# A message-passing kernel whose per-edge products go from split fp32r matmuls to plain fp32 matmuls in four row strips

## The reference

```python
xs = concat([x[src, :8], x[dst, :8]])                  # 16 scalars an edge
xv = concat([x[src, 8:], x[dst, 8:]]).reshape(E, 16, 3)  # 16 vectors an edge
y1, y2 = sph(edge_vec)
h = 2**.5 * relu(emb @ W1 / 10**.5)                    # 10 -> 16
w = (h @ W2 / 16**.5).reshape(E, 7, 16, 8)             # seven 16 x 8 weight blocks of each edge
s_out, g_out, v_out = sums of xs, xv, y1, y2 against the blocks of w
edge_ftr = concat([TG * tanh(s_out), TG * tanh(g_out) * v_out]) * norm
x = layernorm(x + segment_sum(edge_ftr, dst))
x = layernorm(x + attention_sum(x, src, dst))          # second layer
```

## Time and profile before

| | us |
|---|---|
| median of 3 runs | 5801.54 |
| span of the profiled execution | 4918.3 |
| what lies around the span (difference) | 883 |
| TensorE busy, share of the span | 80% |
| VectorE busy | 68% |
| GpSimd busy | 70% |
| ScalarE busy | 34% |

### The profile page before, as it was taken

The page is one execution under the profiler, slowest core; times in us unless marked ns, Lnnn a source line. Parts: engine busy times, 40 slices in busy tenths (PEclk is TensorE's granted clock), DMA queues, the critical chain, the costliest instruction groups (busy, mean ns, idle before and its releaser), DMA issues. The chain is left out here.

```text
span 4918.3 us, 76839 instructions
## 1 busy us (share of the span) xinstructions
PE 3925.7 (80%) x22447; PEld 2433.8 (49%) x22447; DVE 3366.4 (68%) x5756; ACT 1665.0 (34%) x3062; POOL 3457.8 (70%) x3515
## 2 busy tenths in 40 slices
PE   0007999999999999999999600899999999999950
PEld 0004555545544555555555300677777777777740
DVE  4517999999999999999999540455555555555532
ACT  3005666666665666666666300001010100001000
POOL 5777777777666666666663177677777777777766
PEclk9999999999999999999999855899999999999975
DMA  9412222222222222222221000222222222222211
GB/s 327 135 35 50 46 44 45 44 44 46 47 44 43 43 43 43 43 43 43 49 46 30 21 11 14 55 48 46 45 48 48 45 47 49 49 49 49 49 27 25
DMA packets 266830, 253.17 MB, mean 51 GB/s; under 512 B 182298, under 2 KB 237026, under 8 KB 263867
## 3 DMA queue, kind: packets, MB, share of 16 engines
q1 hardware_dynamic: 157118, 174.83, 13.1%
q0 software_dynamic: 109024, 72.30, 9.5%
q10 hardware_dynamic: 462, 4.00, 0.3%
HBM read 160.55 MB, written 90.34 MB: 51 GB/s over the span
## 5 line engine op out<-in xcount | busy, mean ns | idle before, releaser
L626 POOL DMA_INDIRECT edge<-xp_d,idx x1440 | 1437.2, 998 | 634.6 <-issue 358.5
L1231 POOL DMA_INDIRECT gxb<-tab_d,idxb x1200 | 1290.6, 1075 | 376.6 <-issue 324.9
L890 DVE TENSOR_TENSOR prod<-G_ps,hid 128x1000 f32<-128x1000 f32 x1200 | 1385.5, 1192 | 67.0 <-ACT hid L685 39.1
L782 PE MATMUL G_ps<-FT,wst 64*128 64x500 f32 x4800 | 937.9, 434 | 38.2 <-DVE prod L890 38.2
L1266 PE MATMUL G_ps<-tb,hot 125*126 125x500 f32 (+1 forms) x3200 | 675.5, 364 | 333.0 <-DVE hotk L1288 299.7
L792 PE MATMUL R_ps<-prod,red 128*32 128x500 f32 x4800 | 769.4, 601 | 0.0
L1266 PEld LDWEIGHTS G_ps<-tb,hot 125*126 125x126 f32 x3200 | 546.3, 192 | 449.1 <-issue 349.8
L782 PEld LDWEIGHTS G_ps<-FT,wst 64*128 64x128 f32 x4800 | 421.6, 187 | 467.1 <-issue 263.9
L766 PE MATMUL T_ps<-ident,HL 125*128 125x125 f32 x3200 | 519.0, 285 | 129.1 <-DVE HL L880 128.4
L679 ACT ACTIVATE FT<-T_ps 128x500 fp32r<-128x500 f32 x800 | 470.0, 590 | 204.5 <-PE T_ps L766 192.6
L766 PEld LDWEIGHTS T_ps<-ident,HL 125*128 125x128 f32 x3200 | 332.7, 141 | 411.6 <-issue 274.4
(11 more groups left out here) (247 smaller groups left out, 4636.9 us busy)
## 6 DMA issues: line engine op xcount, KB each, us to landing
xd_d<-zeros SPq DMA_DIRECT2D x16, 1562.5 KB, 29.0
y_d<-zrb SPq DMA_DIRECT2D x40, 595.0 KB
edge<-xp_d,idx POOLq DMA_INDIRECT x1440
xv<-xd_d SPq DMA_DIRECT2D x40, 560.0 KB
y_d<-zr SPq DMA_DIRECT2D x40, 560.0 KB
edge<-sel_d SPq DMA_DIRECT2D x40, 546.9 KB
gxb<-tab_d,idxb POOLq DMA_INDIRECT x1200
em<-in_edge_attr SPq DMA_DIRECT2D x40, 175.0 KB
```

Source lines behind the costliest of these rows:

```text
L626: nc.gpsimd.indirect_dma_start(out=edge_c[:, i, 8:8 + DIM], out_offset=None, in_=xp_d, in_offset=bass.IndirectOffsetOnAxis(col, 0)).then_i ...
L782: last = Tn.matmul(G_ps[(k * 3 + i) % 2][:, a * 512:a * 512 + GW], wst[a * 64:(a + 1) * 64, (2 * i + l) * 128:(2 * i + l + 1) * 128], FT[k ...
L890: V.tensor_tensor(prod[k][i][:, :].rearrange("p (a e) -> p a e", a=2), gv, hid[k][:, :].rearrange("p (a e) -> p a e", a=1).broadcast_to([1 ...
L1231: nc.gpsimd.indirect_dma_start(out=gx[h][:, c * T1:(c + 1) * T1], out_offset=None, in_=tab_d, in_offset=bass.IndirectOffsetOnAxis(idx[h][: ...
```

## The change

The products and the MLP layer become plain fp32 matmuls. A transposed group now has 128 rows: four strips of 32, of which the fourth repeats the first input tile (`high` copies three tiles, then tile 0 once more, and `low` is gone). So a group needs four transposes for eight and one copy `out_of_T` for two. The six sets of 32-row products are spread over the strips: `round1` runs four at once, into all four PSUM banks of G_ps; `round2` runs two, into G_ps[0], and may start when multiply 0 has read it. `hidden` uses strip 2 and T_ps[1]. `round1` of a group waits for all three multiplies of the group before. The engines' orders are rewritten around this: TensorE round1(n), reduce(n-1), round2(n), hidden(n+1), back(n-2), transposes(n+2). GpSimd's holds go from four a piece to three. The preparation writes half as many weight columns and no split. The copy of eight index columns at L623 is the same before and after.

```diff
+                    def product(k, r, q, pair, a):
+                        rows = slice(q * KF, (q + 1) * KF)
+                        return Tn.matmul(G_ps[pair][:, a * 512:a * 512 + GW], wst[rows, r * 128:(r + 1) * 128], FT[k][rows, :], start=True, stop=True)
+                    def round1(n, k):
+                        pe.wait_ge(S("b_FT"), n + 1)
+                        if some(n):
+                            pe.wait_ge(S("b_mul"), n * 3)
+                        product(k, 0, 0, 0, 0)
+                        product(k, 0, 1, 0, 1)
+                        product(k, 0, 2, 1, 1)
+                        product(k, 0, 3, 1, 0).then_inc(S("b_G"), 1)
+                    def round2(n, k):
+                        pe.wait_ge(S("b_mul"), n * 3 + 1)
+                        product(k, 1, 0, 0, 0)
+                        product(k, 1, 1, 0, 1).then_inc(S("b_G"), 1)
                     def hidden(n, k):
-                        pe.wait_ge(S("b_FT"), n * NT + 1)
-                        for l in range(2):
-                            last = Tn.matmul(T_ps[0][:, 0:GW], wh[64:128, l * 128:(l + 1) * 128], FT[k][64:128, 0:GW], start=(l == 0), stop=(l == 1))
-                        last.then_inc(S("b_H"), 1)
+                        pe.wait_ge(S("b_FT"), n + 1)
+                        if some(n):
+                            pe.wait_ge(S("b_hid"), n)
+                        Tn.matmul(T_ps[1][:, 0:GW], wst[2 * KF:3 * KF, 128:256], FT[k][2 * KF:3 * KF, :], start=True, stop=True).then_inc(S("b_H"), 1)
...
-                            product(n, k, 2)
-                            if before:
-                                reduce(n - 1, 1 - k)
-                            if more1:
-                                product(n + 1, 1 - k, 0)
-                            if more2:
-                                transposes(n + 2, g2, p2, 0)
-                            if more1:
-                                product(n + 1, 1 - k, 1)
-                            if more2:
-                                transposes(n + 2, g2, p2, 1)
-                            if before:
-                                back(n - 1, 1 - k)
-                            if more2:
-                                hidden(n + 2, k)
+                            round1(n, k)
+                            if not (first and g == 0):
+                                reduce(n - 1, 1 - k)
+                            round2(n, k)
+                            if not (last and g == G2 - 1):
+                                hidden(n + 1, 1 - k)
+                            if not (first and g < 2):
+                                back(n - 2, k)
+                            if not (last and g >= G2 - 2):
+                                transposes(n + 2, g2, p2)
```

VectorE's and ScalarE's part of it:

```diff
                         for d in range(2):
-                            A.activation(HLv[s % 2][:, :, :, 0, d], tiles(s)[:, :, :, d], ACT.Copy).then_inc(S("b_hi"), 1)
+                            A.activation(HLv[s % 2][:, :, 0:3, d], tiles(s)[:, :, :, d], ACT.Copy).then_inc(S("b_hi"), 1)
+                        A.activation(HLv[s % 2][:, :, 3], tiles(s)[:, :, 0], ACT.Copy).then_inc(S("b_hi"), 1)
...
-                        dve.wait_ge(S("b_G"), n * 3 + i + 1)
+                        dve.wait_ge(S("b_G"), n * 2 + (1, 1, 2)[i])
...
+                            scan = None
+                            if gc < 4 and not (last and h == 1):
+                                scan = lambda: fill(gc, ch + 1, 1 - h)
+                            if 4 <= gc < 8 and not (first and h == 0):
+                                scan = lambda: sums(gc - 4, ch - 1, 1 - h)
                             multiply(n, k, 0)
                             multiply(n, k, 1)
+                            if k == 0 and not (first and g < 4):
+                                q = (g - 4) // 2
+                                post(2, t * RING + q, q % RING // PC, q % RING % PC, t if q >= 0 else t - 1)
...
+                            if k == 1 and scan:
+                                scan()
                             multiply(n, k, 2)
+                            if k == 0:
+                                q = (g + 4) // 2
                                 more = not (last and q >= RING)
                                 if more:
+                                    turned(t * RING + q, q % RING, t * 2 + q // PC, q % RING // PC, t + q // RING)
+                                if scan:
+                                    scan()
                                 if more:
+                                    along(t * RING + q, q % RING)
+                            elif not (first and g < 3):
+                                q = (g - 3) // 2
+                                for i in range(2):
+                                    post(i, t * RING + q, q % RING // PC, q % RING % PC, t if q >= 0 else t - 1)
```

More of the change, by code:

```diff
@@ L38, in gnn_resnorm_kernel @@
     EW = 2 * SD
-    NT = 2
+    NR = 2
+    NQ = 4
     SB = 400
@@ L738, in _ @@
                         spread(i, 1, 1, 0)
-                    for n in range(2):
-                        for i in range(NT):
-                            out_of_T(n, n, i)
-                        relu(n, n)
+                    out_of_T(0, 0)
+                    relu(0, 0)
+                    out_of_T(1, 1)
                     turn(0, first=True)
@@ L775, in product @@
-                    def product(n, k, i):
-                        pe.wait_ge(S("b_FT"), n * NT + 2)
-                        if later(n * 3 + i if isinstance(n, int) else n):
-                            pe.wait_ge(S("b_mul"), n * 3 + i - 1)
-                        for l in range(2):
-                            for a in range(2):
-                                c0 = 0 if i == 2 and a == 1 else GW
-                                last = Tn.matmul(G_ps[(k * 3 + i) % 2][:, a * 512:a * 512 + GW], wst[a * 64:(a + 1) * 64, (2 * i + l) * 128:(2 * i + l + 1) * 128],
-                                                 FT[k][a * 64:(a + 1) * 64, c0:c0 + GW], start=(l == 0), stop=(l == 1))
-                        last.then_inc(S("b_G"), 1)
+                    def product(k, r, q, pair, a):
+                        rows = slice(q * KF, (q + 1) * KF)
+                        return Tn.matmul(G_ps[pair][:, a * 512:a * 512 + GW], wst[rows, r * 128:(r + 1) * 128], FT[k][rows, :], start=True, stop=True)
@@ L790, in reduce @@
                         for a in range(2):
-                            for i in range(3):
-                                last = Tn.matmul(R_ps[32 * i:32 * i + 32, 0:GW], red[:, a * KF:(a + 1) * KF], prod[k][i][:, a * GW:(a + 1) * GW], start=(a == 0), stop=(a == 1))
+                            for o in range(3):
+                                i = (o, (0, 2, 1)[o])[a]
+                                last = Tn.matmul(R_ps[32 * o:32 * o + 32, 0:GW], red[:, a * KF:(a + 1) * KF], prod[k][i][:, a * GW:(a + 1) * GW], start=(a == 0), stop=(a == 1))
                         last.then_inc(S("b_R"), 1)
@@ L838, in _ @@
                     reduce(NG - 1, 1)
+                    back(NG - 2, 0)
                     back(NG - 1, 1)
@@ L875, in along @@
                                         AX.X, ALU.add).then_inc(S("b_al"), 1)
-                    def low(p, s):
-                        dve.wait_ge(S("b_hi"), p * 2 + 2)
-                        for d in range(2):
-                            last = V.tensor_tensor(HLv[s % 2][:, :, :, 1, d], tiles(s)[:, :, :, d], HLv[s % 2][:, :, :, 0, d].bitcast(f32), ALU.subtract)
-                        last.then_inc(S("b_lo"), 1)
                     def multiply(n, k, i):
@@ L937, in turn @@
                             ch = t * 2 + h
-                            with_post = k == 1 and not (first and g < 3)
-                            pq = (g - 3) // 2
-                            pm, ps = t * RING + pq, pq % RING
-                            pt = t if pq >= 0 else t - 1
+                            scan = None
[3 more added lines that the diff above has]
+                                scan = lambda: sums(gc - 4, ch - 1, 1 - h)
@@ L983, in _ @@
                         fill(i, 0, 0)
-                    for p in range(3):
+                    for p in range(2):
                         turned(p, p, 0, 0, 0)
                         along(p, p)
-                        if p > 0:
-                            low(p - 1, p - 1)
                     turn(0, first=True)
@@ L992, in _ @@
                     turn(PAIRS - 1, last=True)
+                    post(2, NPIECES - 2, 1, PC - 2, PAIRS - 1)
                     for i in range(3):
```

167 lines of the change are left out of this document (59 added, 108 removed).

## The result

| | before | changed |
|---|---|---|
| median of the timed runs | 5803.35 us (5798.66 to 5805.85) | 5748.66 us (5734.11 to 5772.99) |
| ratio to before, 95% interval | 1 | 0.9919 [0.9894, 0.9945] |
| forecast | | 5732, range 5650 to 5820 |
| span of the profiled execution | 4918.3 us | 5771.2 us |

The change saves 55 us here, 0.9%. Measured again on one chip it took 5757.9 us. The kernel before ran 25 times there, ten times as ctl_before (median 5801.5) and 15 times beside it (5787.7); against all 25 (5794.2) the change saves 36 us, against the ten 44. The sign is the one forecast, the size 21 to 47% short of the 69 us.

The account below looks back on a forecast made before the run. TensorE was taken to set the pace, VectorE close behind; the new VectorE-TensorE chain makes the first message stage 2320 us instead of 2389, saving 69: 5801.5 - 69 = 5732 us, range 5650 to 5820.

Parts of the forecast that it names:

- TensorE's rounds: First message stage: round 1 and round 2 with hidden take 1.06 us each, their strips running side by side.
- Bound 1.90: Upper bound in us for round 1, if its four strips run only two abreast; 1.06 was taken.
- rival B: TensorE's strips run less than abreast; two abreast in round 1 gives 5989 us; chance 0.14 mild, 0.06 hard.
- B mild: Four row strips gain a quarter less than fourfold, streaming 0.84 becomes 1.09 us: 5792 or 5852 us; chance 0.14.
- The chain: First stage: VectorE-TensorE handovers allow a next multiply 2 no sooner than 5.40 us; VectorE's order asks 5.87 after even groups.
- Clock (C): TensorE's new waits in each group lower its clock; every other group would add 320 us, 6052 us; chance 0.08.
- ScalarE's cover: VectorE's 0.6 us wait after post 1 hides ScalarE's 0.2 us lateness for post 0; without it 16 us in all.
- preparation: Block before the message stages: removed copy, splits, DMAs and transposes save 0, bounds 0 and -2 us.
- A: GpSimd's gathers become the first stage's bound at 11.36 us a piece, 162 us less: 5640 us; chance 0.14.
- they keep up, narrowly: GpSimd's gathers in the first stage take 11.36 us a piece, the new consumer 11.60, so gathers do not limit.
- the ring: Buffer of ten gathered pieces in the first stage, claimed to cover a late piece.
- 883 us lie around the span and are kept: Of the runs' median 5801.5 us, all beyond the profiled span of 4918.3 lies outside it and stays unchanged.

Follow-up runs that it names:

- ctl_before: The kernel before, unchanged, run and profiled again on one chip: 5801.52 us, ratio 1.001, profiled span 5789.5 us.
- the undisturbed stage: First message stage with its looped gathers taken out (first ten pieces reused), in both kernels: changed 5028.67 us, before 5135.22 us.
- the five holds: GpSimd holds at columns 1, 2, 4, 5, 6 replacing each kernel's own, column 0 kept: changed kernel 5597.02 us, kernel before 5566.67 us.

## Why the prediction was right, and where it was not

**TensorE's rounds.** Right. Round 1 to reduce 1.05 us (forecast 1.06), round 2 with hidden 1.05, hidden with round 2 and not behind it. Bound 1.90 and rival B fall: rounds of four strips in plain fp32 are fully abreast. The Trainium skill (TensorE: Matmul & The Clock Gate, Part 3, "Measured speedup vs the span model") gives 3.07x for four strips of 32 rows. Laid on the 0.84 of streaming alone, as B mild did, it would have made a round 1.31 us, an estimate; the trace has 1.05. Laid on the whole round it is not far off: four products of 0.84 one behind the other are 3.36, 3.2 times the 1.05.

**The chain.** Right in kind, a little too long: 5.24 for 5.40 after an odd group. Of the 0.16 too much, 0.12 are in the way from multiply 2 to multiply 0 (2.41 for 2.53), and 0.10 of these in the handover from VectorE to TensorE: multiply 2 ends at 1504.91 + 1.17 = 1506.08 and round 1 starts at 1506.13, so 0.05 for 0.15. The even group's 5.87 was 5.86. Without gathers the stage went from 2400.2 to 2285.3, 115 us and not 69: 35 of the 46 more are the new stage (forecast 2320), 11 the old one (2389).

**Clock (C).** Did not come: in the undisturbed stage the granted clock is 0.98 for 0.99. It fell to 0.85 for 0.89 in an ordinary run, and raising it to 0.89 by added work moved nothing.

**ScalarE's cover, preparation.** ScalarE set no pace in the undisturbed trace. The first multiply starts 13 us earlier (428.4 for 441.5), where I had taken 0 to 2 us; with starts between 422.5 and 446.8 us over all profiles of the changed kernel and its variants this is not settled.

**Gathers (A and "they keep up, narrowly").** This is the step that failed. The sum gave GpSimd's holds and gathers a cost of nothing, since the ring covers a late one. It did cover them: VectorE's turned step waits for no gather. What they cost is TensorE's late signals: 636 us of the stage before (3036.1 - 2400.2) and 728 after (3013.5 - 2285.3). The changed kernel pays 92 us more, and of the 115 us that its shorter chain gains 23 are left in the stage.

**"883 us lie around the span and are kept."** Wrong. 1.8 us lie around the changed kernel's span (5772.99 - 5771.2) and some 2 around the second profile of before. The 871 us were inside: 659 in the first stage, 172 behind it, 40 ahead. The page's execution and the runs' median were different executions, and a sum that subtracts a saving read in the one from the time of the other assumes that the saving carries over. By the number it carried over by 53 to 79% (36 and 55 of 69 us), but through two errors against each other: the undisturbed gain is 106.5 us and not 69 (115 in the stage), and 52 to 70 us are lost with the late signals. That the forecast of 5732 lies within 17 us of 5748.66 is therefore luck; the chain that it was made from is not.

What is shown: the gathers bring the late signals on (none without them, hardly any cost with half); with all gathers made, the holds decide their cost (some 370 us from two holds less, 161 and 235 us gained with the five); VectorE's order doesn't matter while they are there. What is argued: that the changed kernel pays more because its TensorE now waits for all three multiplies and then VectorE for TensorE, so that a late signal anywhere stops both, where the kernel before had one product ahead. The pair with five holds fits this, but no run kept the new rounds and gave back the lead. What is open: how a gather delays TensorE's signals, or its matmuls; why one profiled execution was free of it; what the holds change; and why the kernel before ran at 5709 us once. The length of a burst does not order the runs: 7.8 and 7.9 gathers between two stops go with 5796 and 6132 us, 5.4 and 5.6 with 5758 and 5597, and 31.5 with the execution that had no late signal.

## What to carry to other kernels

Compare the profiled span with the median before anything is summed. A gap of 15% is another regime and not overhead, and a saving read in the quiet execution must be weighed against what limits the ordinary one. Where GpSimd gathers without a pause beside three engines that hand work to each other every microsecond, try first where its holds stand: here that was worth 3 to 4%, and the whole change to the products under 1%. A change that removes slack between two engines may make each disturbance dearer (argued here, not shown), so its gain should be measured again after the disturbance is mended: with the five holds this one was 30 us slower than the kernel before.

## What the runs showed of the hardware that I had not expected

- TensorE's signals can arrive 2 to 4 us late at VectorE and ScalarE while GpSimd issues gathers, with all three idle (1497.5 to 1499.8 above); theirs did not (none of 4148). Four gathers a piece, GpSimd busy 731 of 2000 us, cost 27 us; eight cost 729.
- Waits that only hold GpSimd back make the kernel before 4% and the changed one 2.8% faster; taking two away makes the changed one some 6% slower.
- Four row strips of 32, each plain fp32 with 500 columns, take 1.05 us, as long as a round of two product strips and hidden.
- The profiled execution of a kernel can be 15% shorter than each of its timed runs (4918.3 against 5798.66 to 5805.85 us).
